# Constant tails of the packed queries and keys written by ScalarE instead of five DMAs, in the three cross attentions of a twelve-layer network

## The chip, the cores and the metric

The kernel runs on one core of one Trainium2 chip. The metric is the device time of one execution in microseconds (us), the median of several runs. A profile of one execution shows when each instruction of each engine ran: TensorE (PE in the rows, its weight loads PEld), VectorE (DVE), ScalarE (ACT), GpSimd (POOL), and the queue of SyncE (SPq), which only issues DMAs here. ScalarE can issue DMAs too (ACTq).

## The reference, cut to what matters

A perceiver: 128 latent rows `x` of 256 columns pass through twelve layers. Three of them (L0, L1, L3) are cross attentions of 16 heads over 12,544 context rows; the other nine aren't touched by the change.

```python
# a cross attention (L0_xattn; L1 adds a mask on the keys, L3 a rotation of the queries)
q = split_heads(x_q @ Wq + bq) * dp_scale        # x_q: layer norm of x, 128 rows, 16 heads of 16
k = split_heads(x_kv @ Wk + bk)                  # x_kv: ctx_1024, 12544 rows
v = split_heads(x_kv @ Wv + bv)
attn = jnp.einsum('bhic,bhjc->bhij', q, k)
attn = jnp.where(causal_mask, neg, attn)
attn = jax.nn.softmax(attn, axis=-1)
o = jnp.einsum('bhij,bhjc->bhic', attn, v)
```

## The kernel before, in words

**Chunks and steps.** `CrossAttention` walks the context in 49 chunks of 256 keys (`NCHUNK`), in 56 steps (`STEPS`). At step `s` the engines project chunk `s` to keys and values. The maxima of the scores of chunk `s - 1` are found from a coarse product. The real scores of chunk `s - 6` (`LAG` is 6) are computed and exponentiated. So the first six steps, 0 to 5, hold projection and maxima only: I call them the run-up. From step 6 on the full loop runs. Step 5 ends with the first shift (minus the maxima), which TensorE turns (line 952) and SyncE sends into the packed queries; the first real score (line 938) stands behind it.

**One step of the run-up**, by engine and line:
- TensorE: the coarse scores of the chunk before (line 889, two batches `d` of 0 and 1), the projection to keys (854), the projection to values (858). The order is batch 0, keys, batch 1, values.
- ScalarE: `act_drain_k` (1099) writes the projected keys with their bias from PSUM to `k_full`; `act_drain_v` (1111) the values; `act_round_context` (1164) rounds the context of chunk `s + 3`; then in steps 0 and 1 `act_low_queries` (1172), in step 2 `act_copy_queries` (1180). In the masked layer L1 the keys are drained by VectorE (1368) instead.
- GpSimd: `split_keys` (1260 high half, 1262 low half), `split_context` (1245, low half of the context).
- VectorE: four reductions (1326) of 1024 columns each; at step 5 `update_shift` (1335 to 1341).
- SyncE: `load_context` (679) of chunk `s + 3`; from step 1 `pack_keys` (691 and 694), eight DMAs that lay the high and low halves of a chunk's keys one below the other in partitions 0 to 95 of one of three buffers `k_packed`; in steps 3 and 4 `pack_queries` (745, 746) for `q_packed`.

**Queues.** Each engine runs its instructions in the order of the code, and a wait holds up everything behind it on that engine. The context load of step 2 stands on SyncE behind the eight `pack_keys` issues of step 1, and those stand behind everything of step 0. On ScalarE the rounding of step 2 (line 1164) waits for the context that this load brings, and the key drain of step 3 stands behind it.

**The tails.** The packed tiles have 128 partitions, and the products use all of them. Partitions 96 and 97 of the queries hold the two parts of the shift; the other rows from 96 on are zero in the queries, while those of the keys are one, so that the product adds the shift. In L1, rows 98 and 99 carry the mask. `fill_tails` (line 721) writes partitions 96 to 127 of both `q_packed` and all three `k_packed` once per layer, by five DMAs of 256 KB from the constants in SBUF, at step 0, after the context load of that step. `pack_keys` and, in L1, `fill_queries` wait on SyncE until all five have landed (`tails_filled` at 80).

Of the kernel before, what the change touches and what calls it, by code (L numbers as in the profile page):

```python
# [8 lines left out]
ACT = mybir.ActivationFunctionType  # L9
F32 = mybir.dt.float32  # L10
# [6 lines left out]
P = 128  # L17
# [4 lines left out]
H = 16  # L22
# [288 lines left out]
def times(ap, m):  # L311

    return ap.unsqueeze(1).broadcast_to([ap.shape[0], m, ap.shape[1]])
# [248 lines left out]
def block_turned(step):  # L562

    return next((b for b in range(BLOCKS) if turn_step(b) == step), None)
# [49 lines left out]
class CrossAttention:  # L614
# [67 lines left out]
    def pack_keys(self, sp, m, quarter):  # L682

        L, s = self.L, m % 3
        if quarter == 0:
            sp.wait_ge(L["k_lo_ready"], m + 1)
            sp.wait_ge(L["tails_filled"], 80)
        if m >= 3:
            sp.wait_ge(L["e_filled"], E_AT["scores", m - 3, 4 + quarter] + 1)
        own = slice(32 * quarter, 32 * quarter + 32)  # L690
        sp.dma_start(self.k_packed[s][0:32, quarter, :, :].rearrange("p d t -> p (d t)").bitcast(F32),
                     self.k_ring[own, m % K_RING, 0, :, :].rearrange("p d t -> p (d t)").bitcast(F32))\
          .then_inc(L[f"packed{s}_{quarter}"], 16)
        sp.dma_start(self.k_packed[s][32:96, quarter, :, :].rearrange("p d t -> p (d t)").bitcast(F32),
                     self.k_ring[own, m % K_RING, :, :, :].rearrange("p a d t -> p a (d t)").bitcast(F32))\
          .then_inc(L[f"packed{s}_{quarter}"], 16)

    def load_key_mask(self, act, m):

        L, s = self.L, m % 3  # L700
        row = self.mask_dram[1:2, m * KEYS:(m + 1) * KEYS].unsqueeze(1).broadcast_to([2, H // 2, KEYS])
        act.dma_start(self.k_packed[s][98:100, :, :, :].rearrange("p q d t -> p (q d) t").bitcast(F32), row)\
           .then_inc(L[f"key_mask_loaded{s}"], 16)
# [10 lines left out]
    def load_shift(self, sp, b):  # L714

        L = self.L
        sp.wait_ge(L["e_drained"], E_AT["turned", b] + 1)
        sp.dma_start(self.q_packed[b % 2][96:98, :, :].bitcast(F32), self.stage_T[32:64, :].bitcast(F32))\
          .then_inc(L["shift_loaded"], 16)

    def fill_tails(self, sp):

        L, tail = self.L, slice(96, P)
        self.wait_first(sp)
        for c in range(2):
            sp.dma_start(self.q_packed[c][tail, :, :].bitcast(F32), times(self.net.const("fill")[tail, :], H))\
              .then_inc(L["tails_filled"], 16)
        for c in range(3):
            sp.dma_start(self.k_packed[c][tail, :, :, :].rearrange("p q d t -> p (q d t)")
                         .rearrange("p (a n) -> p a n", n=P).bitcast(F32), times(self.net.const("ones")[tail, :], H))\  # L730
              .then_inc(L["tails_filled"], 16)

    def pack_queries(self, sp, quarter):

# [13 lines left out]
    def fill_queries(self, sp):  # L748

        L = self.L  # L750
        if self.masked:
            sp.wait_ge(L["tails_filled"], 80)
            sp.dma_start(self.q_packed[0][98:100, :, :].bitcast(F32), times(self.net.const("fill")[0:2, :], H))\
              .then_inc(L["q_packed_ready"], 16)
            sp.dma_start(self.q_packed[1][98:100, :, :].bitcast(F32), times(self.net.const("fill")[0:2, :], H))\
              .then_inc(L["q_repeated"], 16)
# [17 lines left out]
    def sync(self, sp):  # L774
        L, ins = self.L, self.net.ins
# [12 lines left out]
        for step in range(STEPS):  # L788
            m, b = step - LAG + 2, block_turned(step)
            if step + 3 < NCHUNK and step < LAG + 2:  # L790
                self.load_context(sp, step + 3)
            if step == 0:
                self.fill_tails(sp)
            if step == 1:
                self.fill_queries(sp)
            if 1 <= step < 3:
# [117 lines left out]
    def pe_unit(self, pe, m, u):  # L914
# [3 lines left out]
        L, s, half, quarter = self.L, m % 3, u // 4, u % 4  # L918
        unit = E_AT["scores", m, u]
        bank = E_BANK[unit]  # L920
        q = self.q_packed[m // BLOCK % 2]
        if u == 0 and m % BLOCK == 0:
            pe.wait_ge(L["shift_loaded"], 16 * (m // BLOCK + 1))
        if u == 0 and m == BLOCK:
            pe.wait_ge(L["q_repeated"], 32 if self.masked else 16)
        if half == 0:
# [255 lines left out]
    def scalar(self, act):  # L1182
        L = self.L
# [6 lines left out]
            self.act_split_weights(act)  # L1190
        for n in range(3):
            self.act_round_context(act, n)
        if self.masked:
            act.wait_ge(L["mask_stored"], 32)
            self.load_mask(act, 0)
            self.load_mask(act, 1)
        for step in range(STEPS):
            m = step - LAG
# [24 lines left out]
                self.act_low_queries(act, step)  # L1223
            if step == DC:
                self.act_copy_queries(act)
        self.attended.scalar(act)

    def gpsimd(self, pool):
# [1606 lines left out]
```

## Time and profile before

| | |
|---|---|
| median of three runs | 1681.87 us |
| the three runs | 1680.31 to 1682.96 us |
| the profiled execution | 1682.3 us |
| its span in the trace | 1680.5 us (1.8 us lie around it) |
| TensorE busy | 1583.4 us, 94% of the span |
| first real score of L0, L1, L3 | at 48.03, 562.02, 1235.35 us of the span |

The page of the profile gives busy time by engine over the whole span. For a change at the start of three layers the timeline, which lists the instructions of each engine in order of time with the idle time ahead of them and what ended it, is the view to read; the table of stretches gives for each stretch the busy time of the engines and the TensorE clock that was granted.

### The profile page before, as it was taken

To read this page: it belongs to the slowest core of one execution; us is meant where nothing else is said; L and a number is where in the kernel's file an instruction comes from. 1 tells how busy PE (TensorE), PEld (TensorE's weight loads), DVE (VectorE), ACT (ScalarE), POOL (GpSimd) and SP (SyncE) were. 2 spreads that over 40 slices of the span, in tenths; PEclk is the share of its full clock that TensorE was granted. 3 is DMA by queue.
4 is the path that set the end of the run, shared out by engine and by line. 5 is a ranking of instruction groups with operands and counts; after the bars stand their busy time and mean duration, and the time that the engine had idled before them with its cause. 6 is when DMAs were issued, how large, how long until landed. Compare 5 with 4: busy or idle time off the path is not lost. (4 is left out here: it accounts for less than half of the span.)

```text
span 1680.5 us, 48975 instructions
## 1 busy us (share of the span) xinstructions
PE 1583.4 (94%) x20179; PEld 1368.8 (81%) x20179; DVE 1045.0 (62%) x1445; ACT 948.5 (56%) x1812; POOL 693.4 (41%) x627
## 2 busy tenths in 40 slices
PE   7999999999887999999999988998799999999988
PEld 6898888888666889999999775996578998999863
DVE  6667787885346777777777343045676666666622
ACT  3677777777412466666666722352257777777742
POOL 5655555551004645555554000000375555555202
PEclk9999999999978899999999999989999999999997
DMA  6675565554235766555565352970475555655430
GB/s 179 169 194 136 122 139 135 132 124 106 62 116 116 186 184 164 148 144 139 139 150 126 85 208 100 348 274 34 117 183 141 141 128 121 142 133 130 106 105 4
DMA packets 149248, 235.65 MB, mean 140 GB/s; under 512 B 24200, under 2 KB 64516, under 8 KB 148100
## 3 DMA queue, kind: packets, MB, share of 16 engines
q1 hardware_dynamic: 141090, 225.29, 51.4%
q10 hardware_dynamic: 7938, 7.23, 1.7%
q8 instruction: 163, 2.67, 0.7%
q14 instruction: 57, 0.47, 0.1%
HBM read 107.26 MB, written 0.23 MB: 64 GB/s over the span
## 5 line engine op out<-in xcount | busy, mean ns | idle before, releaser
L1326 DVE TENSOR_REDUCE L_xattn_maxima<-L_xattn_ps 128x4 f32<-128x1024 f32 x588 | 691.3, 1219 | 318.7 <-PE L_xattn_ps L889 314.8
L1086 ACT ACTIVATE L_xattn_p_ring<-L_xattn_ps 128x512 f32<-128x512 f32 x1176 | 673.7, 598 | 335.2 <-PE L_xattn_ps L938 319.8
L938 PE MATMUL L_xattn_ps<-L_xattn_q_packed,L_xattn_k_packed 128*128 128x256 f32 x2352 | 450.6, 297 | 5.2 <-ACT L_xattn_p_ring L1086 4.7
L938 PEld LDWEIGHTS L_xattn_ps<-L_xattn_q_packed,L_xattn_k_packed 128*128 128x128 f32 x2352 | 336.2, 190 | 59.5 <-issue 35.9
L980 PE MATMUL L_xattn_ps<-L_xattn_p_ring,L_xattn_v_ring 128*17 128x128 f32 x9408 | 289.3, 273 | 1.0 <-ACT L_xattn_p_ring L1086 1.0
L858 PE MATMUL L_xattn_ps<-L_xattn_w_halves,L_xattn_ctx_halves 128*128 128x256 f32 x1764 | 266.5, 287 | 0.4 <-ACT L_xattn_k_full L1099 0.4
L854 PE MATMUL L_xattn_ps<-L_xattn_ctx_halves,L_xattn_w_halves 128*128 128x256 f32 x1764 | 262.9, 288 | 1.0 <-POOL L_xattn_ctx_halves L1245 1.0
L980 PEld LDWEIGHTS L_xattn_ps<-L_xattn_p_ring,L_xattn_v_ring 128*17 128x17 f32 x9408 | 242.4, 97 | 23.5 <-ACT L_xattn_p_ring L1086 1.6
L1242 POOL TENSOR_TENSOR L_xattn_ctx_halves<-L_xattn_ctx_chunk,consts 128x512 fp32r<-128x512 f32 x129 | 134.2, 1041 | 270.8 <-DMA L_xattn_ctx_chunk<-in_ctx_chunks 192.7
L1260 POOL TENSOR_TENSOR L_xattn_k_ring<-L_xattn_k_full,consts 128x512 fp32r<-128x512 f32 x147 | 153.9, 1047 | 210.4 <-ACT L_xattn_k_full L1099 105.2
L854 PEld LDWEIGHTS L_xattn_ps<-L_xattn_ctx_halves,L_xattn_w_halves 128*128 128x128 f32 x1764 | 235.2, 195 | 4.0 <-issue 1.8
L858 PEld LDWEIGHTS L_xattn_ps<-L_xattn_w_halves,L_xattn_ctx_halves 128*128 128x128 f32 x1764 | 234.8, 193 | 2.6 <-ACT L_xattn_k_full L1099 0.6
L1245 POOL TENSOR_TENSOR L_xattn_ctx_halves<-L_xattn_ctx_chunk,L_xattn_ctx_halves 128x512 fp32r<-128x512 f32 x147 | 189.6, 1290 | 18.4 <-ACT L_xattn_ctx_halves L1164 8.2
L1262 POOL TENSOR_TENSOR L_xattn_k_ring<-L_xattn_k_full,L_xattn_k_ring 128x512 fp32r<-128x512 f32 x147 | 189.5, 1289 | 11.5
L889 PE MATMUL L_xattn_ps<-L_xattn_k_ring,L_xattn_q_hi 32*128 32x256 f32 x2352 | 148.9, 311 | 9.8 <-issue 4.2
L889 PEld LDWEIGHTS L_xattn_ps<-L_xattn_k_ring,L_xattn_q_hi 32*128 32x128 f32 x2352 | 109.6, 185 | 43.3 <-issue 17.8
L1111 ACT ACTIVATE L_xattn_v_ring<-L_xattn_ps 128x512 f32<-128x512 f32 x147 | 87.8, 597 | 51.4 <-PE L_xattn_ps L858 39.8
L1099 ACT ACTIVATE L_xattn_k_full<-L_xattn_ps,weights 128x256 f32<-128x256 f32 x196 | 81.6, 471 | 18.3 <-PE L_xattn_ps L854 18.3
L243 POOL TENSOR_SCALAR L_attn_rstd<-L_attn_mean_var 128x1 f32<-128x1 f32 x4 | 0.9, 221 | 174.3 <-DVE L_attn_mean_var L232 174.3
L1356 DVE TENSOR_TENSOR L_xattn_ps<-L_xattn_ps,L_xattn_factor 128x512 f32<-128x512 f32 x36 | 24.8, 690 | 50.7 <-PE L_xattn_ps L980 50.7
L884 PE MATMUL L_xattn_ps<-L_xattn_fill_rows,L_xattn_fill_terms 2*128 2x512 f32 x392 | 52.5, 501 | 3.6 <-DVE L_xattn_maxima L1326 1.6
L1368 DVE SCALAR_TENSOR_TENSOR L_xattn_k_full<-L_xattn_ps,weights,L_xattn_mask_chunk 128x256 f32<-128x256 f32 x98 | 42.6, 476 | 1.9 <-PE L_xattn_ps L854 1.5
(387 smaller groups left out, 1174.7 us busy)
## 6 DMA issues: line engine op xcount, KB each, us to landing
L_xattn_k_packed<-L_xattn_k_ring SPq DMA_DIRECT2D x588, 128.0 KB, 2.4
L_xattn_ctx_chunk<-in_ctx_chunks SPq DMA_DIRECT2D x147, 256.0 KB, 3.1
L_xattn_k_packed<-L_xattn_k_ring SPq DMA_DIRECT2D x588, 64.0 KB, 2.2
L_ffn_W<-in_experts_W SPq DMA_DIRECT2D x16, 1024.0 KB, 11.8
L_xattn_mask_chunk<-L_xattn_mask ACTq DMA_DIRECT2D x49, 128.0 KB, 3.0
weights<-in_pack_L_attn SPq DMA_DIRECT2D x10, 512.0 KB, 4.9
L_xattn_ctxT<-in_ctxT SPq DMA_DIRECT2D x5, 896.0 KB, 12.9
L_xattn_ctx<-in_ctx SPq DMA_DIRECT2D x5, 896.0 KB, 11.6
```

Of the source, the lines that this page charges most:

```text
L854: last = pe.matmul(L.ps[:, KV_BANK, d * KEYS:(d + 1) * KEYS], wk[:, b, e, d * P:(d + 1) * P], x[:, a, e, :], start=start, stop=stop, skip_ ...
L858: last = pe.matmul(L.ps[:, self.v_bank(n), t * D:(t + 1) * D], x[:, a, e, t * P:(t + 1) * P], wv[:, b, e, :], start=start, stop=stop, skip ...
L889: last = pe.matmul(bank[:, r, k * KEYS:(k + 1) * KEYS], self.q_hi[own, 2 * d + k, :], self.k_ring[own, slot, 0, d, :], start=not self.mask ...
L938: last = pe.matmul(L.ps[:, bank, d * 2 * S:(d + 1) * 2 * S], self.k_packed[s][:, quarter, d, half * P:(half + 1) * P], q[:, 2 * pair:2 * p ...
L980: last = pe.matmul(L.ps[q:q + DH + 1, ACC_BANK, col:col + S], self.v_ring[:, m % V_RING, half, h, :], self.p[t % P_RING][:, at, :], start= ...
L1086: act.activation(self.p[t % P_RING][:, 4 * quarter:4 * quarter + 4, :], L.ps[:, E_BANK[unit], :].rearrange("p (h n) -> p h n", n=S), ACT.Exp)\
L1111: act.activation(self.v_ring[:, n % V_RING, :, :, 0:DH].rearrange("p t h n -> p (t h) n"), L.ps[:, self.v_bank(n), :].rearrange("p (m n) - ...
L1242: pool.tensor_tensor(hi, self.ctx_chunk[c][:, :, :], wide(ones[:, 0:DC], KEYS), ALU.mult)\
L1245: pool.tensor_tensor(lo, self.ctx_chunk[c][:, :, :], hi.bitcast(F32), ALU.subtract)\
L1260: pool.tensor_tensor(hi, k[:, :, :], wide(ones[:, 0:DC], KEYS), ALU.mult).then_inc(L["k_hi_ready"], 1)
L1262: pool.tensor_tensor(lo, k[:, :, :], hi.bitcast(F32), ALU.subtract).then_inc(L["k_lo_ready"], 1)
L1326: dve.tensor_reduce(out[:, 4 * v:4 * v + 4], L.ps[:, M_BANK + 2 * v:M_BANK + 2 * v + 2, :] .rearrange("p b (k n) -> p (b k) n", k=2), AX_X ...
```

## The change

The five DMAs of `fill_tails` are gone. ScalarE writes the same constants: `fill_query_tails` issues two ACTIVATEs (Copy with scale 0.0, so zeros) of 32 partitions by 2048 elements after the three roundings that stand ahead of the steps, and `fill_key_tails` one (Copy of ones) of the same size at the end of steps 1, 2 and 3. `tails_filled` now counts to 5 by ones. `pack_keys` no longer waits for it, since it writes other partitions. The wait has moved to TensorE's first real score, to `load_shift` and `fill_queries` on SyncE (2, the queries alone) and, in L1, to `load_key_mask` on ScalarE.

```diff
     def pack_keys(self, sp, m, quarter):
         if quarter == 0:
             sp.wait_ge(L["k_lo_ready"], m + 1)
-            sp.wait_ge(L["tails_filled"], 80)
...
     def load_key_mask(self, act, m):
+        act.wait_ge(L["tails_filled"], 5)
...
     def load_shift(self, sp, b):
         sp.wait_ge(L["e_drained"], E_AT["turned", b] + 1)
+        sp.wait_ge(L["tails_filled"], 2)
...
-    def fill_tails(self, sp):
+    def fill_query_tails(self, act):
         L, tail = self.L, slice(96, P)
-        self.wait_first(sp)
         for c in range(2):
-            sp.dma_start(self.q_packed[c][tail, :, :].bitcast(F32), times(self.net.const("fill")[tail, :], H))\
-              .then_inc(L["tails_filled"], 16)
-        for c in range(3):
-            sp.dma_start(self.k_packed[c][tail, :, :, :].rearrange("p q d t -> p (q d t)")
-                         .rearrange("p (a n) -> p a n", n=P).bitcast(F32), times(self.net.const("ones")[tail, :], H))\
-              .then_inc(L["tails_filled"], 16)
+            act.activation(self.q_packed[c][tail, :, :], times(self.net.const("ones")[tail, :], H), ACT.Copy, scale=0.0)\
+               .then_inc(L["tails_filled"], 1)
+
+    def fill_key_tails(self, act, c):
+        L, tail = self.L, slice(96, P)
+        act.activation(self.k_packed[c][tail, :, :, :].rearrange("p q d t -> p (q d t)").rearrange("p (a n) -> p a n", n=P),
+                       times(self.net.const("ones")[tail, :], H), ACT.Copy).then_inc(L["tails_filled"], 1)
...
     def fill_queries(self, sp):
         if self.masked:
-            sp.wait_ge(L["tails_filled"], 80)
+            sp.wait_ge(L["tails_filled"], 2)
...
     def sync(self, sp):
-            if step == 0:
-                self.fill_tails(sp)
...
     def pe_unit(self, pe, m, u):
+        if u == 0 and m == 0:
+            pe.wait_ge(L["tails_filled"], 5)
...
     def scalar(self, act):
         for n in range(3):
             self.act_round_context(act, n)
+        self.fill_query_tails(act)
...
             if step == DC:
                 self.act_copy_queries(act)
+            if 1 <= step < 4:
+                self.fill_key_tails(act, step - 1)
```

On SyncE, from the context loads at the start of L0 to the first packed keys, before:

```order
L679 DMA L_xattn_ctx_chunk<-in_ctx_chunks 128x512 [waits L0_xattn_ctx_split]
L726 DMA L_xattn_q_packed<-consts 32x16x128 [waits x_and_consts_loaded]
L726 DMA L_xattn_q_packed<-consts 32x16x128
L729 DMA L_xattn_k_packed<-consts 32x16x128 x3
L679 DMA L_xattn_ctx_chunk<-in_ctx_chunks 128x512 [waits L0_xattn_ctx_split]
L691 DMA L_xattn_k_packed<-L_xattn_k_ring 32x512 [waits L0_xattn_tails_filled,L0_xattn_k_lo_ready]
```

The same place on SyncE now (first line: the loads of steps 0 and 1):

```order
L679 DMA L_xattn_ctx_chunk<-in_ctx_chunks 128x512 [waits L0_xattn_ctx_split] x2
L690 DMA L_xattn_k_packed<-L_xattn_k_ring 32x512 [waits L0_xattn_k_lo_ready]
L693 DMA L_xattn_k_packed<-L_xattn_k_ring 64x1x512
L690 DMA L_xattn_k_packed<-L_xattn_k_ring 32x512
L693 DMA L_xattn_k_packed<-L_xattn_k_ring 64x1x512
```

Five issues and one wait have left the stretch between the context loads and the packing of the first keys.

On ScalarE, from the value drain of step 1 to the key drain of step 3 of L0 (1111 drains values, 1164 rounds context, 1172 and 1180 prepare the queries, 1099 drains keys), before:

```order
L1111 ACTIVATE L_xattn_v_ring<-L_xattn_ps 128x32x16 [waits L0_xattn_v_in_psum]
L1164 ACTIVATE L_xattn_ctx_halves<-L_xattn_ctx_chunk 128x512 [waits L0_xattn_v_in_psum,L0_xattn_ctx_loaded1]
L1172 ACTIVATE L_xattn_p_ring<-L_xattn_p_ring,consts 128x128 [waits L0_xattn_q_lo_ready]
L1172 ACTIVATE L_xattn_p_ring<-L_xattn_p_ring,consts 128x128
L1099 ACTIVATE L_xattn_k_full<-L_xattn_ps,weights 128x256 [waits L0_xattn_k_lo_ready,L0_xattn_k_in_psum]
L1099 ACTIVATE L_xattn_k_full<-L_xattn_ps,weights 128x256
L1111 ACTIVATE L_xattn_v_ring<-L_xattn_ps 128x32x16 [waits L0_xattn_v_in_psum]
L1164 ACTIVATE L_xattn_ctx_halves<-L_xattn_ctx_chunk 128x512 [waits L0_xattn_v_in_psum,L0_xattn_ctx_loaded2]
L1180 ACTIVATE L_xattn_p_ring<-L_xattn_q_hi 128x512 [waits L0_xattn_q_heads_ready]
L1099 ACTIVATE L_xattn_k_full<-L_xattn_ps,weights 128x256 [waits L0_xattn_k_lo_ready,L0_xattn_k_in_psum]
```

The same stretch now (its line numbers are two higher):

```order
L1113 ACTIVATE L_xattn_v_ring<-L_xattn_ps 128x32x16 [waits L0_xattn_v_in_psum]
L1166 ACTIVATE L_xattn_ctx_halves<-L_xattn_ctx_chunk 128x512 [waits L0_xattn_v_in_psum,L0_xattn_ctx_loaded1]
L1174 ACTIVATE L_xattn_p_ring<-L_xattn_p_ring,consts 128x128 [waits L0_xattn_q_lo_ready]
L1174 ACTIVATE L_xattn_p_ring<-L_xattn_p_ring,consts 128x128
L732 ACTIVATE L_xattn_k_packed<-consts 32x2048
L1101 ACTIVATE L_xattn_k_full<-L_xattn_ps,weights 128x256 [waits L0_xattn_k_lo_ready,L0_xattn_k_in_psum]
L1101 ACTIVATE L_xattn_k_full<-L_xattn_ps,weights 128x256
L1113 ACTIVATE L_xattn_v_ring<-L_xattn_ps 128x32x16 [waits L0_xattn_v_in_psum]
L1166 ACTIVATE L_xattn_ctx_halves<-L_xattn_ctx_chunk 128x512 [waits L0_xattn_v_in_psum,L0_xattn_ctx_loaded2]
L1182 ACTIVATE L_xattn_p_ring<-L_xattn_q_hi 128x512 [waits L0_xattn_q_heads_ready]
L732 ACTIVATE L_xattn_k_packed<-consts 32x2048
L1101 ACTIVATE L_xattn_k_full<-L_xattn_ps,weights 128x256 [waits L0_xattn_k_lo_ready,L0_xattn_k_in_psum]
```

A tail (line 732) now stands between the work on the queries and the key drain, at the end of steps 1 and 2; a third one stands at the end of step 3, and two (line 726) ahead of the key drain of step 0.

## Rows read from the trace of the kernel before

**Rows 1.** Page: busy time by engine over the span.

```profile
PE 1583.4 (94%) x20179; PEld 1368.8 (81%) x20179; DVE 1045.0 (62%) x1445; ACT 948.5 (56%) x1812; POOL 693.4 (41%) x627
```

**Rows 2.** Stretches (busy us by engine, then granted TensorE clock): L0, L1, L3.

```profile
32.00:37.00 5.00, 1.99 (x20) 1.89 (x20) 1.45 (x2) 2.27 (x5) 3.06 (x3) 0.98 0.77 185
37.00:42.00 5.00, 5.00 (x25) 4.37 (x25) 4.65 (x7) 1.19 (x3) 4.05 (x5) 0.50 0.83 190
63.00:71.00 8.00, 8.00 (x122) 7.26 (x122) 4.79 (x5) 5.85 (x12) 4.46 (x4) 1.00 0.76 189
...
557.00:562.00 5.00, 5.00 (x32) 4.47 (x29) 3.26 (x3) 0.60 (x1) 4.84 (x5) 0.50 0.62 159
...
1227.00:1232.00 5.00, 3.54 (x33) 3.09 (x33) 3.96 (x7) 1.71 (x4) 4.83 (x5) 1.00 0.71 166
```

**Rows 3.** Timeline, L0 (start, duration, instruction, idle before): SyncE, and VectorE's reductions.

```profile
13.06 5.05 SPq L729 DMA_DIRECT2D L_xattn_k_packed<-consts  x3
...
17.18 4.62 DVE L1326 TENSOR_REDUCE L_xattn_maxima<-L_xattn_ps 128x4 f32<-128x1024 f32 x4 [0.40 <-PE L_xattn_ps L889]
...
22.88 0.57 SPq L691 DMA_DIRECT2D L_xattn_k_packed<-L_xattn_k_ring  x1
...
28.80 0.58 SPq L679 DMA_DIRECT2D L_xattn_ctx_chunk<-in_ctx_chunks  x1
...
35.55 2.35 DVE L1326 TENSOR_REDUCE L_xattn_maxima<-L_xattn_ps 128x4 f32<-128x1024 f32 x2 [3.71 <-PE L_xattn_ps L889]
```

**Rows 4.** Timeline, L0: ScalarE's drains and roundings, GpSimd's split, the first score.

```profile
14.29 0.84 ACT L1099 ACTIVATE L_xattn_k_full<-L_xattn_ps,weights 128x256 f32<-128x256 f32 x2 [3.13 <-PE L_xattn_ps L854]
...
16.58 1.35 POOL L1262 TENSOR_TENSOR L_xattn_k_ring<-L_xattn_k_full,L_xattn_k_ring 128x512 fp32r<-128x512 f32 x1
...
31.91 0.63 ACT L1164 ACTIVATE L_xattn_ctx_halves<-L_xattn_ctx_chunk 128x512 fp32r<-128x512 f32 x1 [4.54 <-DMA L_xattn_ctx_chunk<-in_ctx_chunks]
...
32.97 0.82 ACT L1099 ACTIVATE L_xattn_k_full<-L_xattn_ps,weights 128x256 f32<-128x256 f32 x2
...
48.03 0.40 PE L938 MATMUL L_xattn_ps<-L_xattn_q_packed,L_xattn_k_packed 128*128 128x256 f32 x2
```

**Rows 5.** Groups by line and shape, ScalarE: the same copy at two sizes.

```profile
L1164 ACT ACTIVATE L_xattn_ctx_halves<-L_xattn_ctx_chunk 128x512 fp32r<-128x512 f32 x18 | 10.8, 625 | 12.4 <-DMA L_xattn_ctx_chunk<-in_ctx_chunks 12.3
L1842 ACT ACTIVATE L_xattn_ctx_parts<-L_xattn_ctx 128x1792 fp32r<-128x1792 f32 x5 | 8.5, 1694 | 6.4 <-PE L_xattn_ps L1885 3.6 <-DMA L_xattn_ctx<-in_ctx 2.7
```

**Rows 6.** Timeline, L3: ScalarE, VectorE's reductions of steps 1 and 4, the first score.

```profile
1198.54 1.66 ACT L1164 ACTIVATE L_xattn_ctx_halves<-L_xattn_ctx_chunk 128x512 fp32r<-128x512 f32 x3
...
1205.00 0.84 ACT L1099 ACTIVATE L_xattn_k_full<-L_xattn_ps,weights 128x256 f32<-128x256 f32 x2 [4.81 <-PE L_xattn_ps L854]
...
1207.64 4.62 DVE L1326 TENSOR_REDUCE L_xattn_maxima<-L_xattn_ps 128x4 f32<-128x1024 f32 x4 [1.70 <-PE L_xattn_ps L889]
...
1213.23 0.68 ACT L1172 ACTIVATE L_xattn_p_ring<-L_xattn_p_ring,consts 128x128 f32<-128x128 f32 x2
...
1220.02 0.63 ACT L1164 ACTIVATE L_xattn_ctx_halves<-L_xattn_ctx_chunk 128x512 fp32r<-128x512 f32 x1 [2.19 <-DMA L_xattn_ctx_chunk<-in_ctx_chunks]
...
1223.65 4.62 DVE L1326 TENSOR_REDUCE L_xattn_maxima<-L_xattn_ps 128x4 f32<-128x1024 f32 x4 [1.37 <-PE L_xattn_ps L889]
...
1235.35 0.40 PE L938 MATMUL L_xattn_ps<-L_xattn_q_packed,L_xattn_k_packed 128*128 128x256 f32 x2
```

**Rows 7.** Timeline, L1: mask load behind queued work, value drain, VectorE's chain.

```profile
521.31 0.38 ACT L259 ACTIVATE L_xattn_xnT<-L_xattn_ps 128x256 f32<-128x256 f32 x1 [3.94 <-PE L_xattn_ps L252]
521.33 0.35 ACTq L710 DMA_DIRECT2D L_xattn_mask_chunk<-L_xattn_mask  x1
...
526.30 0.86 DVE L1368 SCALAR_TENSOR_TENSOR L_xattn_k_full<-L_xattn_ps,weights,L_xattn_mask_chunk 128x256 f32<-128x256 f32 x2
...
527.77 0.60 ACT L1111 ACTIVATE L_xattn_v_ring<-L_xattn_ps 128x512 f32<-128x512 f32 x1 [4.52 <-PE L_xattn_ps L858]
...
544.75 4.61 DVE L1326 TENSOR_REDUCE L_xattn_maxima<-L_xattn_ps 128x4 f32<-128x1024 f32 x4
```

## The prediction, made before the changed kernel ran

> **What bounds the kernel now.** TensorE is busy 94% of the span [rows 1]. In the full loop it has no gap: 8.00 of 8.00 us at full clock in the stretch from 63 us [rows 2]. A change that only touches the run-up of a layer can't shorten that loop. It can only let it begin earlier, and the loop then carries the shift to its end, since nothing in it stands on a fixed time. So the measure is the time of the first real score of each of the three layers, and I read the timeline backwards from it.
>
> The views in their order. First the timeline of VectorE. In the run-up a step takes 5.02 us, 4.62 of reductions and 0.40 for the turn to the next batch [rows 3]. I call the start of a step's first reduction t1 (step 1) to t4 (step 4). In L0, t1 is 17.18 and t4 would be 17.18 + 3 x 5.02 = 32.24, but it is 35.55, after 3.71 us of idle time. Then the timeline of ScalarE: it stood 4.54 us until 31.91, waiting for a context load, and only then came to the key drain of step 3, at 32.97 [rows 4]. From the start of that drain to t4 it is 35.55 - 32.97 = 2.58 us (drain, split on GpSimd, coarse product). Then the timeline of SyncE, for why the load was late: it was issued at 28.80, behind eight packing issues that began only at 22.88, though their keys were ready at 16.58 + 1.35 = 17.93 [rows 3, 4]. What they waited for were the five tail DMAs, whose last three took SyncE from 13.06 to 18.11 to issue, and then had to land.
>
> L3 shows the same in small: 2.19 us of waiting for the load, and 1.37 us of idle ahead of t4 in place of 0.40 [rows 6]. In L1 nothing of it reaches VectorE. Its row at 544.75 has no idle time ahead of it [rows 7], because there VectorE drains the keys itself and is the slowest engine of the step.
>
> **What is removed.** Packing of the first keys can start at about 18 instead of 22.88, and the context load behind it moves as much, from 28.80 to about 23.9; with the 3.1 us between issue and use (28.80 to 31.91) it is there at 27.0. ScalarE asks for it at about 27.7 (below), so this wait goes altogether. In L3 the load moves alike. Left alone, the removal would bring t4 in L0 to 32.24, 3.3 us earlier, and in L3 by 1.37 - 0.40 = 1.0 us.
>
> **What is added: five ACTIVATEs per layer.** No row has one of 2048 elements per partition. The nearest are the same SBUF copy at 1792 (1694 ns) and at 512 (625 ns) [rows 5]: 0.835 ns an element, so 1.694 + 256 x 0.835/1000 = 1.91 us each. Bounds: 1.69 below (the row of 1792) and, if a source that repeats 128 elements or a write to 32 partitions ran at half the rate, 3.8 above. I take 1.91, because cost follows the elements per partition in every ScalarE row. Queued ones overlap: three of 0.62 take 1.66 [rows 6], so 0.09 to 0.10 each.
>
> *The two query tails*, ahead of the first key drain: 2 x 1.91 less three overlaps is 3.55 us. ScalarE was idle there for 3.13 in L0, 4.52 in L1 and 4.81 in L3 [rows 4, 6, 7]. L1 and L3 hide them; in L0 they delay the key drain of step 0, and with it t1, by 0.42, to 17.60.
>
> *The key tail of step 1.* The work on the queries ends at t1 + 6.27 (1213.91 - 1207.64 in L3) [rows 6]. The tail runs from t1 + 6.18 to t1 + 8.09, and the key drain of step 2 starts at t1 + 8.00 at the earliest, with t3 = t1 + 8.00 + 2.58 = t1 + 10.58. Undisturbed it would be t1 + 10.04. So this tail costs 0.54 in both layers, where keys are drained by ScalarE.
>
> *The key tail of step 2.* The same sum with one copy of 512 elements (0.62, as in [rows 5]) where two short ones (0.68) stood gives the drain of step 3 at t2 + 7.94, and t4 no earlier than t2 + 10.52 = t1 + 15.54. The other path is t3 + 5.02 = t1 + 15.60. The second decides, so this tail is hidden, by 0.06 only. *That of step 3* ends about t4 + 1.8, when the next keys just come out of TensorE: 0 to 0.2, and the drain of step 4 has slack there. I take 0.
>
> Together t4 is t1 + 15.60: in L0 17.60 + 15.60 = 33.20, 2.35 earlier than 35.55. In L3 it is 1207.64 + 15.60 = 1223.24, 0.41 earlier than 1223.65.
>
> **From t4 to the first score.** It took 48.03 - 35.55 = 12.48 us in L0 [rows 3, 4] and 1235.35 - 1223.65 = 11.70 in L3 [rows 6]. The difference is TensorE's clock: after the gap in L0 (1.99 busy of 5 us) it was granted half, 1.2 GHz, for the stretch from 37 us, while L3 stayed at 2.4 GHz with 3.54 busy of 5 at worst [rows 2]. With the gap gone the run-up of L0 looks like that of L3, so I take 11.70: another 0.78 us. Bounds: 0 and 0.78.
> The Trainium skill, in TensorE: Matmul & The Clock Gate, section HAM oscillation, says that waits for data between groups of matmuls bring the slow clock back. By that rule too the 0.78 comes with the gap. L1 speaks against counting on it: it had half clock from 557 to 562 us [rows 2] without a late load on VectorE's path, which is a rival below.
>
> **The moved waits** cost nothing. The third key tail ends near 35 in L0, and TensorE's first score, which waits for it, comes at 45; `load_shift` asks for the query tails, done at about 14.8. The ScalarE wait in L1 is on its own earlier writes. Five issues fewer on SyncE give slack and no time in L1.
>
> **L1** by itself: its query tails end before the value drain at 527.77 wants ScalarE. Its mask loads are issued by ScalarE behind them, though. They were issued at 521.33, 0.02 us after the first of four queued ACTIVATEs began [rows 7]. So the sequencer runs at least four ahead. If it ran no further, two more would hold the issue until the second of them is done, at about 522.2: 0.9 late. The mask was wanted at 526.30. With 0.35 of issue and the 3.1 us that the larger context load took to be used, it is there at about 525.7. So 0, with a bound of 0.9.
> The Trainium skill, in Advanced Engine Details and Errata, section Engine Queue Depths, gives eight entries for ScalarE. By it the six ACTIVATEs fit and the issue isn't held at all; no row here shows more than four.
>
> **The sum.** L0 2.35 + 0.78 = 3.13; L3 0.41; L1 0. That is 3.5 us, from the profiled 1682.3 us to 1678.8. This execution was 0.4 above the median of 1681.87, so the median goes to 1678.4. Own range of this case: 2.7 to 4.5 saved, 1677.4 to 1679.2.
>
> **Rivals.**
> (a) *The clock falls anyway, somewhere else in L0's run-up*, as it did in L1. A stretch of 5 us at half clock, all busy, holds 2.5 us of work at full clock [rows 2], so up to 2.5 of the 3.5 are lost, in the middle 1.9: 1680.3. For it: TensorE still waits for the shift in step 5. Against it: L3 has the same wait and kept its clock.
> (b) *The first score comes earlier but the loop doesn't.* Something else, such as SyncE's packing in steps 5 to 8, sets the loop's start. Then 0 to 0.8 saved, about 1681.5. Against it: the stretch from 63 us has no gap on TensorE, and SyncE gains slack.
> (c) *Slower: a tail takes far longer than its elements say.* The place is ScalarE in steps 0 to 2 of L0 and L3. With T for one tail, L0's t1 moves by 2 (T - 1.91) and t4 by 3 (T - 1.91); L3's t4 by 1 (T - 1.91) while its query tails are hidden. The gain of 3.5 is eaten at 4 (T - 1.91) = 3.5, so at T = 2.8. At T = 3.8 it is 3.5 - 4 x 1.9 = -4.1 and about 1 more because L3's query tails come out of cover: 1687. Against it: no ScalarE row is slower than by its elements. For it: no row has this shape.
> (d) *More is saved:* the tails run nearer 1.69, or the freed DMA traffic speeds the rest. t3 in both layers then gains 0.2, t1 in L0 0.4, and all of the removal would come through at most: 3.3 + 0.78 + 1.0 = 5.1, 1676.8.
>
> **How the numbers follow.** Forecast 0.62, (a) 0.13, (b) 0.10, (c) 0.07, (d) 0.08. The range leaves out (c) and the ends of (b) and (d): 1676.9 to 1681.8. A measurement of this kernel tells about 0.2%, 3.4 us, from no change, so the line is at 1678.5, in the middle of my forecast. Faster by more than that: half of the forecast, a little over, and (d), 0.42. Slower: (c) and a trace of noise, 0.08. Within 0.2%: the rest, 0.50.
>
> **What would show it.** In L0: rows of line 726 and 732 of 1.9 us each; key drain of step 0 at 14.7; no wait of ScalarE for a context load; t3 near 28.2 (0.54 later than two undisturbed steps after t1), t4 near 33.2, full clock from 37 to 42 us, first score at 44.9. In L3: t4 0.4 us earlier counted from the layer's start. In L1: the first score as long after the layer's start as before. I am wrong if a tail isn't near 1.9 us, if L0's first score comes before 43.5 or after 46, or if the full loop begins to show gaps on TensorE.

## The result, and the profile after

The changed kernel takes 1676.22 us in the median of 20 runs, beside 1681.64 us for the kernel before on the same chip: ratio 0.9976, 95% interval 0.9968 to 0.9984, which is 4.0 us less (2.7 to 5.4; the two medians alone lie 5.4 us apart, at the edge of that). Timed again later it was 1676.31 us beside 1680.47, ratio 0.9970 (0.9959 to 0.9981). The forecast was 3.5 us less. On the median of 1681.87 us from which it was made, the first ratio gives 1677.8 us, in the range; the raw median lies 0.7 us below the range's low end. The profiled span is 1673.7 us.

The page has fewer packets and bytes (149248 and 235.65 MB before), and more of ScalarE than in [rows 1]:

```profile
PE 1579.2 (94%) x20179; PEld 1364.2 (82%) x20179; DVE 1037.2 (62%) x1445; ACT 977.5 (58%) x1827; POOL 694.1 (41%) x627
...
DMA packets 141328, 231.72 MB, mean 138 GB/s; under 512 B 23960, under 2 KB 56596, under 8 KB 140180
```

ScalarE's timeline in L0 (start, duration, instruction, idle before it), to be laid beside [rows 4]. L726 are the query tails, L732 the key tails, L1101 the key drains, L1166 the rounding of the context:

```profile
10.69 3.72 ACT L726 ACTIVATE L_xattn_q_packed<-consts 32x2048 fp32r<-32x2048 f32 x2
14.43 0.84 ACT L1101 ACTIVATE L_xattn_k_full<-L_xattn_ps,weights 128x256 f32<-128x256 f32 x2
...
22.35 0.62 ACT L1166 ACTIVATE L_xattn_ctx_halves<-L_xattn_ctx_chunk 128x512 fp32r<-128x512 f32 x1
...
23.57 1.91 ACT L732 ACTIVATE L_xattn_k_packed<-consts 32x2048 fp32r<-32x2048 f32 x1
25.51 0.84 ACT L1101 ACTIVATE L_xattn_k_full<-L_xattn_ps,weights 128x256 f32<-128x256 f32 x2
...
27.35 0.62 ACT L1166 ACTIVATE L_xattn_ctx_halves<-L_xattn_ctx_chunk 128x512 fp32r<-128x512 f32 x1
...
28.51 1.91 ACT L732 ACTIVATE L_xattn_k_packed<-consts 32x2048 fp32r<-32x2048 f32 x1
30.45 0.84 ACT L1101 ACTIVATE L_xattn_k_full<-L_xattn_ps,weights 128x256 f32<-128x256 f32 x2
```

Each key tail is 1.91 us, the two query tails 3.72 together. The rounding at 27.35 has no idle time ahead of it, where 4.54 us stood before. Now VectorE in L0, beside [rows 3]; the last four rows are the reduction of the maxima and the three small operations of the first shift:

```profile
17.29 4.62 DVE L1331 TENSOR_REDUCE L_xattn_maxima<-L_xattn_ps 128x4 f32<-128x1024 f32 x4 [1.59 <-PE L_xattn_ps L889]
22.29 4.63 DVE L1331 TENSOR_REDUCE L_xattn_maxima<-L_xattn_ps 128x4 f32<-128x1024 f32 x4 [0.38 <-PE L_xattn_ps L889]
28.11 4.62 DVE L1331 TENSOR_REDUCE L_xattn_maxima<-L_xattn_ps 128x4 f32<-128x1024 f32 x4 [1.19 <-PE L_xattn_ps L889]
33.11 4.62 DVE L1331 TENSOR_REDUCE L_xattn_maxima<-L_xattn_ps 128x4 f32<-128x1024 f32 x4 [0.38 <-PE L_xattn_ps L889]
37.76 0.30 DVE L1340 TENSOR_REDUCE L_xattn_maxima<-L_xattn_maxima 128x16 f32<-128x80 f32 x1
38.10 0.49 DVE L1344 TENSOR_SCALAR L_xattn_stage<-L_xattn_maxima 128x16 fp32r<-128x16 f32 x1
38.62 0.97 DVE L1345 SCALAR_TENSOR_TENSOR L_xattn_stage<-L_xattn_maxima,L_xattn_stage 128x16 fp32r<-128x16 f32 x1
39.62 0.18 DVE L1346 TENSOR_TENSOR L_xattn_shift<-L_xattn_stage 128x16 f32<-128x16 f32 x1
```

The four first rows are t1 to t4. The 3.71 us ahead of t4 are gone; 1.19 us stand ahead of t3 in their place, 0.8 more than the usual 0.38. TensorE's clock (the figure right behind the five counts, 1.00 is 2.4 GHz) stays up where [rows 2] had 0.50, and the first score of L0 comes at 44.14 us instead of 48.03:

```profile
32.00:37.00 5.00, 4.82 (x43) 4.07 (x42) 4.62 (x5) 3.35 (x4) 3.79 (x4) 1.00 0.82 183
37.00:42.00 5.00, 4.17 (x39) 3.74 (x37) 3.94 (x7) 1.71 (x4) 4.78 (x5) 1.00 0.22 67
```

In L3 the first score comes 39.76 us after the layer's first context load is issued (1190.67 to 1230.43), before 40.53 (1194.82 to 1235.35). The two run-ups together give 3.89 + 0.77 = 4.66 us. The spans differ by more, 6.8 us. Of the other 2.1 us, 1.34 lie in L1's run-up and the rest in stretches that the change doesn't touch. The next table shows how far both wander: e5, whose L1 has the code of the kernel before, has a run-up of 44.10 us there, not 45.50.

The table holds the time from a layer's first context load to its first score, for L0 from the start of the span, and the two long stretches between the run-ups (first score of L0 to L1's first load, first score of L1 to L3's). All in us, from the traces:

| kernel | L0 t1 | L0 t4-t1 | L0 first score | L1 run-up | L3 run-up | L0 to L1 | L1 to L3 | ratio to before |
|---|---|---|---|---|---|---|---|---|
| before | 17.18 | 18.37 | 48.03 | 45.50 | 40.53 | 468.5 | 632.8 | 1 |
| changed | 17.29 | 15.82 | 44.14 | 44.16 | 39.76 | 468.2 | 634.1 | 0.9976 |
| changed, again | 17.81 | 15.83 | 44.65 | 44.09 | 39.33 | 468.8 | 633.2 | 0.9970 |
| e1 | 17.68 | 16.26 | 45.62 | 43.95 | 38.58 | 467.4 | 634.6 | 0.9975 |
| e2 | 17.21 | 15.00 | 44.92 | 44.53 | 39.43 | 470.5 | 631.6 | 0.9981 |
| e3 | 17.76 | 15.01 | 43.50 | 46.80 | 38.56 | 468.8 | 633.1 | 0.9965 |
| e4 | 17.34 | 19.02 | 47.45 | 44.05 | 42.75 | 469.4 | 633.2 | one run |
| e5 | 17.13 | 18.01 | 46.85 | 44.10 | 40.71 | 467.7 | 634.8 | one run |
| e6 | 17.04 | 15.04 | 42.80 | 45.22 | 38.57 | 469.1 | 633.0 | 0.9969 |
| e7 | 17.53 | 15.84 | 43.60 | 41.70 | 37.87 | 467.9 | 632.3 | 0.9936 |
| e10 | 17.30 | 15.03 | 42.39 | 42.18 | 36.93 | 468.2 | 632.5 | 0.9930 |
| e11 | 17.32 | 19.10 | 47.33 | 42.97 | 38.70 | 467.3 | 636.0 | 0.9963 |

### The profile page after: what moved, and what is told of

Same layout as the page of the kernel before. It is cut to its first block and busy times, and to the rows that moved or that the text cites. A ratio compares the mean times of both kernels' runs of the same rounds, so it can differ in the third digit from the quotient of the medians.

```text
span 1673.7 us, 49007 instructions
## 1 busy us (share of the span) xinstructions
PE 1579.2 (94%) x20179; PEld 1364.2 (82%) x20179; DVE 1037.2 (62%) x1445; ACT 977.5 (58%) x1827; POOL 694.1 (41%) x627
## 5 line engine op out<-in xcount | busy, mean ns | idle before, releaser
L1101 ACT ACTIVATE L_xattn_k_full<-L_xattn_ps,weights 128x256 f32<-128x256 f32 x196 | 81.8, 472 | 6.2 <-PE L_xattn_ps L854 6.0
```

## The experiments

**The wait or the transfers: e1.** The kernel before, with the wait moved and the five DMAs left where they were.

```diff
     def pack_keys(self, sp, m, quarter):
         if quarter == 0:
             sp.wait_ge(L["k_lo_ready"], m + 1)
-            sp.wait_ge(L["tails_filled"], 80)
...
     def pe_unit(self, pe, m, u):
+        if u == 0 and m == 0:
+            pe.wait_ge(L["tails_filled"], 80)
```

> The kernel before with the five tail DMAs where they were, but the wait for them taken from pack_keys and put where the changed kernel has it: ahead of the first real score on TensorE, of load_shift and of the key-mask loads. ScalarE writes nothing. Theory (what cost the kernel before its time was the wait for the DMAs to land, at one place of SyncE's queue): pack_keys of chunk 0 starts near 18 us in L0, the context load of step 2 near 23, ScalarE's rounding doesn't wait, t3 is t1+10.04, t4 is t1+15.06 (32.2), the first score of L0 comes near 43.2 us (the changed kernel: 44.14), and the time is 1 to 2 us below the changed kernel's, about 1675 us. Rival (the five transfers themselves, 2.5 times the bytes of a pack, crowd the queues and the packed copies that come after): SyncE's issues stretch from 0.6 towards 2 us each, the context load of step 2 lands late all the same, t4 stays over 33, and the time is between the two kernels', 1678 to 1681 us.

Measured: 1676.22 us, ratio 0.9975 (0.9960 to 0.9990), the same as the changed kernel's. My theory had the time nearly right and the trace of L0 wrong. There t4 is t1 + 16.26, against 18.37 before and 15.06 undisturbed, so the wait cost 2.1 us, and with the DMAs still there another 1.2 stayed. SyncE's and ScalarE's timelines in L0 show where:

```profile
11.41 1.41 SPq L727 DMA_DIRECT2D L_xattn_q_packed<-consts  x2
12.86 5.01 SPq L730 DMA_DIRECT2D L_xattn_k_packed<-consts  x3
17.91 1.59 SPq L679 DMA_DIRECT2D L_xattn_ctx_chunk<-in_ctx_chunks  x1
19.54 1.53 SPq L690 DMA_DIRECT2D L_xattn_k_packed<-L_xattn_k_ring  x1
...
24.94 2.15 SPq L693 DMA_DIRECT2D L_xattn_k_packed<-L_xattn_k_ring  x1
```

```profile
23.22 0.63 ACT L1167 ACTIVATE L_xattn_ctx_halves<-L_xattn_ctx_chunk 128x512 fp32r<-128x512 f32 x1 [0.38 <-DMA L_xattn_ctx_chunk<-in_ctx_chunks]
...
30.30 0.63 ACT L1167 ACTIVATE L_xattn_ctx_halves<-L_xattn_ctx_chunk 128x512 fp32r<-128x512 f32 x1 [2.45 <-DMA L_xattn_ctx_chunk<-in_ctx_chunks]
```

Issues that take 0.6 us elsewhere take about 1.5 to 1.8 here up to 21.1 us, and one takes 2.15 at 24.94. The context load of step 2 is issued at 27.13, beside 23.16 in the changed kernel, and ScalarE still waits 2.45 us for it. The first part of this stands while the tails are in flight. The last of them landed at 22.40, though, and a long issue near this place is in every L0: 1.45 us at 25.41 in the kernel before, 1.25 us at 26.26 in the changed kernel, where it stands behind the context load and delays nothing that is waited for. So the 1.2 us came with the DMAs, but how much of it their transfers made and how much the long issue that now fell ahead of the load isn't shown. In L3 t4 is t1 + 15.04: there the DMAs cost nothing, while ScalarE's tails cost the changed kernel 0.8 us. The first score of L0 comes 1.5 us later than in the changed kernel and that of L3 1.2 us earlier, which fits two equal times.

**Later DMAs for the keys: e2.** Query tails on ScalarE, key tails by DMA in step 3.

```diff
+            if step == 3:
+                self.fill_key_tails(sp)
...
-            if 1 <= step < 4:
-                self.fill_key_tails(act, step - 1)
```

> The changed kernel with the query tails on ScalarE as they are, but the three key tails fetched by DMAs again, issued by SyncE in step 3 behind that step's query packing, and waited for only at the first real score and the key-mask loads. Theory (each key tail on ScalarE pushes the K drain of the next step; in the changed kernel the one of step 1 costs 0.78 us in L0 and in L3): the VectorE idle of 1.19 us ahead of t3 falls to 0.38, t4 is t1+15.06 (32.4), the DMAs issue at about 32 to 34 us and land by 41, and the first score of L0 comes near 43.4. L3 gains as much. Time 1.5 us below the changed kernel's, about 1674.7. Rival (the late DMAs delay the query packing's landing or the context loads behind them, and the first score waits for them): first score of L0 at 44 or later, time that of the changed kernel or up to 1 us above it.

Measured: 1676.82 us, ratio 0.9981 (0.9966 to 0.9997). The first half of the theory held: t4 is t1 + 15.00, no idle ahead of t3. Then the rival did. TensorE's timeline of L0, key projection and first score:

```profile
43.27 0.74 PE L858 MATMUL L_xattn_ps<-L_xattn_ctx_halves,L_xattn_w_halves 128*128 128x256 f32 x4 [0.81 <-DMA L_xattn_q_packed<-L_xattn_p_ring]
44.92 0.79 PE L944 MATMUL L_xattn_ps<-L_xattn_q_packed,L_xattn_k_packed 128*128 128x256 f32 x2 [0.91 <-DMA L_xattn_q_packed<-L_xattn_stage_T]
```

```profile
42.00:47.00 5.00, 3.28 (x17) 2.87 (x18) 2.17 (x2) 0.60 (x1) 4.72 (x5) 0.69 0.75 173
47.00:52.00 5.00, 4.98 (x26) 4.23 (x26) 2.35 (x2) 3.01 (x6) 2.32 (x2) 0.50 0.89 224
```

The packed queries land late behind the tails, TensorE waits twice, and the clock falls to 0.50 behind that. So step 3 isn't a free place for these transfers either; others weren't tried.

**Another place for the key tails: e3 and e6.** e3 puts them behind the key drain of the same step in all layers, e6 in L0 and L3 alone.

```diff
             self.act_drain_k(act, step)
+            if 1 <= step < 4:
+                self.fill_key_tails(act, step - 1)
             self.act_unit(act, m, 2)
```

> The changed kernel with the three key tails still on ScalarE in steps 1, 2 and 3, but right behind the K drain of the step, ahead of its V drain, where ScalarE of L0 sat idle for 2.09 us in step 1 (19.76 to 21.85), and no longer behind the rounding of the context. Theory (an ACTIVATE of 1.91 us costs what it pushes, and here it fits the gap): the K drain of step 2 starts near 24.0, t3 is t1+10.04 with 0.38 us of idle ahead of it, t4 is t1+15.06 (32.4), the first score of L0 near 43.4, and L3 gains 0.75 us as well; time about 1674.7 us, 1.5 below the changed kernel's. Rival (the V drain comes later by what the tail overruns the gap, and the rounding and the V projection behind it are late instead): t3 as in the changed kernel, t1+10.8, and a time within 0.5 us of the changed kernel's.

> The key tails behind the K drain of steps 1, 2 and 3 in L0 and L3, as in e3_tails_after_drain, but in the masked layer L1 where the changed kernel has them, behind the rounding of the context. Theory (in e3_tails_after_drain the place gained 1.0 us or so in L0 and L3 against the changed kernel, t3 and t4 without idle, and lost in L1, where VectorE waited 1.33 us for TensorE after 529 us, because the V drain stood behind the tail): first score of L0 near 43.2 to 43.6, L3 start to first score 38.6, L1 start to first score 44.2 to 45.5 instead of 46.80, and a time 0.5 to 1.5 us below that of e3_tails_after_drain, about 1674.3. Rival (L1's longer run-up was made by the clock, which dips there in every kernel, and is given back later): L1's pace of reductions is regular, yet the time is that of e3_tails_after_drain within its interval.

Measured: e3 1675.15 us, ratio 0.9965 (0.9952 to 0.9978); e6 1674.79 us, 0.9969 (0.9957 to 0.9981). In both, t4 is t1 + 15.0 in L0 and the L3 run-up is 38.6 instead of 39.76: the 1.91 us of ACTIVATE fit the gap between key and value drain, and the 0.8 us that the tail of step 1 had pushed is back; another 0.3 lies behind t4 and is explained below. In L1, e3 does cost VectorE a wait (1.33 us at 532.96), and e6 has its even pace again. The time didn't follow: e6's clock in L1 stayed low longer (0.50 and 0.59 in 552 to 562 us), its run-up took 45.22, and the ratios are the same within their intervals. The rival on L1 holds as far as these traces go. Against the changed kernel neither place is a difference that the intervals settle.

**Longer tails: e4.** Each key tail written twice.

```diff
                 self.fill_key_tails(act, step - 1)
+                act.wait_ge(self.L["tails_filled"], 2 * step + 1)
+                self.fill_key_tails(act, step - 1)
```

> The changed kernel with each key tail written twice in a row on ScalarE, so that its cost is 3.8 us instead of 1.91. Theory (the tail of step 1 is at the edge of its cover and every further microsecond of steps 1 and 2 goes to VectorE's period): L0 t3 is 1.9 us later against t1 than in the changed kernel (t1+12.7), t4 3.8 later (t1+19.6), the first score 3.8 to 5.7 later (48 to 50 us); in L3 t4 is later by 1.9 to 3.8. Time 7 to 11 us above the changed kernel's, 1683 to 1687. Rival (there is cover left in steps 2 and 3, VectorE's reductions and the clock set the pace): t4 is less than 2.5 us later and the time stays under 1681.

Measured: 1682.97 us in one run. In L0 t3 is t1 + 12.76, 1.94 later than in the changed kernel, as expected. t4 is t1 + 19.02, 3.20 later and not 3.8, and the first score 3.31. In L3 the first score is 2.99 later, in L1 not at all. That is 6.3 us of run-ups; the one run is 6.8 us above the changed kernel's median. The tail of step 1 has no cover left, and that of step 2 some 0.6 us: ScalarE had been idle for 0.50 us between the two, ahead of the value drain at 26.85.

**The clock: e5.** The kernel before with 13 matmuls of zeros in the gap of L0.

```diff
             if step < LAG - 1:
+                if step == 4 and self.first:
+                    L.keep_busy(pe, E_BANKS[0], 13)
                 self.pe_batch(pe, step, 0)
```

> The kernel before, tails by DMA and the wait in pack_keys as they were, with 13 further matmuls of zeros (128x512, into a free PSUM bank, their result unused) on TensorE in step 4 of L0 alone, ahead of that step's first batch, where TensorE of the kernel before sat idle for 3.25 us (31.75 to 35.01). Theory (0.8 us of what the changed kernel gained in L0 is TensorE's clock, which fell to 0.50 in 37 to 42 us after that idle): t4 stays near 35.5, granted clock 1.00 in 37 to 42 and 42 to 47, the first score of L0 comes near 47.2 us instead of 48.03. Rival (the clock doesn't matter there, since VectorE and the shift set the pace): full clock, but the first score still at 48.0 within 0.2.

TensorE's stretches in L0:

```profile
32.00:37.00 5.00, 4.92 (x36) 3.08 (x34) 1.86 (x2) 2.09 (x6) 3.46 (x3) 1.00 0.79 178
37.00:42.00 5.00, 3.73 (x32) 3.22 (x28) 4.86 (x7) 2.06 (x5) 4.25 (x5) 1.00 0.75 177
```

Full clock, and from t4 (35.14) to the first score (46.85) 11.71 us instead of 12.48. The clock was worth 0.77 us. The further 0.41 us by which the score is early came with t4; the wait for the context load was 0.35 us shorter in this trace. The one run took 1681.33 us, which doesn't tell 1.2 us from none.

**What the sum didn't have: e7, e11.** After e5 one thing was open. The clock explains 12.48 to 11.71, but the changed kernel takes 11.03 in L0 and 11.02 in L3, where the clock was full before as well and it took 11.70. GpSimd's timeline of the changed kernel in L0, against the VectorE rows above:

```profile
37.27 1.29 POOL L1267 TENSOR_TENSOR L_xattn_k_ring<-L_xattn_k_full,L_xattn_k_ring 128x512 fp32r<-128x512 f32 x1
38.52 1.04 POOL L1247 TENSOR_TENSOR L_xattn_ctx_halves<-L_xattn_ctx_chunk,consts 128x512 fp32r<-128x512 f32 x1
39.64 1.30 POOL L1250 TENSOR_TENSOR L_xattn_ctx_halves<-L_xattn_ctx_chunk,L_xattn_ctx_halves 128x512 fp32r<-128x512 f32 x1
```

L1344 began at 38.10 and ended at 38.59, GpSimd's first one here at 38.56. L1345 began at 38.62, 0.10 after GpSimd's next, and ended at 39.59, that one at 39.56. Both take 0.17 to 0.20 alone. The kernel before had the same, with other partners:

```profile
40.83 0.89 DVE L1339 TENSOR_SCALAR L_xattn_stage<-L_xattn_maxima 128x16 fp32r<-128x16 f32 x1
41.76 0.17 DVE L1340 SCALAR_TENSOR_TENSOR L_xattn_stage<-L_xattn_maxima,L_xattn_stage 128x16 fp32r<-128x16 f32 x1
41.97 1.14 DVE L1341 TENSOR_TENSOR L_xattn_shift<-L_xattn_stage 128x16 f32<-128x16 f32 x1
```

GpSimd's operations there ran 40.65 to 41.69 and 41.77 to 43.08. A small VectorE operation of this kind that begins while GpSimd works on a tensor ends with GpSimd's. The reduction L1340 doesn't: it ran 37.76 to 38.06 beside GpSimd's first one and took 0.30. The Trainium skill, in SBUF — State Buffer, section Who interferes with whom, has this as a rule: the two engines share a pair of ports, a VectorE instruction with two SBUF inputs or in a two-port mode needs it, and the later one blocks for the whole of the other. The rows here agree: L1345, with two inputs, and L1344 were held, the reduction with its one input wasn't. Which mode L1344 ran in no row tells. e7 takes the overlap of L1345 away in the changed kernel, e11 those in the kernel before:

```diff
         for step in range(NCHUNK):
             if step < LAG:
                 split_keys(step)
+                if step == LAG - 2:
+                    pool.wait_ge(L["stage_ready"], 1)
                 split_context(step + 2)
```

> The changed kernel with one wait more: GpSimd doesn't begin the split of context chunk 6 (in step 4 of each layer) before VectorE's shift of block 0 is done. In all traces so far a small operation of that shift (128x16, 0.17 to 0.20 us alone) that met a GpSimd tensor operation ended with it: in the changed kernel L1345 ran 38.62 to 39.59 and GpSimd's 38.52 to 39.56. Theory (a VectorE operation of this kind waits until GpSimd's has ended, and this is the term that made the end of the run-up 0.7 us shorter than figured): L1345 takes 0.17 to 0.2, the shift 1.2 to 1.3 us instead of 2.04 in L0 and 2.05 in L3, the first scores come 0.7 to 0.8 earlier against t4 in both (10.3 instead of 11.03), GpSimd's split starts 0.3 to 0.5 later, and the time is 1 to 1.5 us below the changed kernel's, about 1674.9. Rival (GpSimd's later split delays the keys of chunk 5 and the context, or something else stretches the small operations): the first score comes as late as in the changed kernel, 44.1, and the time is the same or 0.5 us more.

> The kernel before with nothing but the added wait of e7_gpsimd_after_shift: GpSimd begins the split of context chunk 6 when the shift of block 0 is done. Theory (the collision of VectorE's small operations with GpSimd's is a cost of its own, which was there before the change and depends only on how the two engines happen to line up): the shift of L0 takes near 1.0 to 1.3 us instead of 2.61, that of L3 as much instead of 2.63, both first scores come 1.3 to 1.6 us earlier (L0 near 46.5, L3 start to first score near 39.0), the clock of L1 stays at 1.00 and its start to first score is 41.7 instead of 45.5, and the time is 5.5 to 7 us below that of the kernel before, about 1675. Rival (the gain of the added wait needs the changed kernel's timing): less than 3 us of gain.

VectorE, then GpSimd, in L0 of e7:

```profile
38.35 0.49 DVE L1346 TENSOR_SCALAR L_xattn_stage<-L_xattn_maxima 128x16 fp32r<-128x16 f32 x1
38.88 0.17 DVE L1347 SCALAR_TENSOR_TENSOR L_xattn_stage<-L_xattn_maxima,L_xattn_stage 128x16 fp32r<-128x16 f32 x1
39.09 0.17 DVE L1348 TENSOR_TENSOR L_xattn_shift<-L_xattn_stage 128x16 f32<-128x16 f32 x1
```

```profile
39.34 1.04 POOL L1247 TENSOR_TENSOR L_xattn_ctx_halves<-L_xattn_ctx_chunk,consts 128x512 fp32r<-128x512 f32 x1 [0.53 <-DVE L_xattn_shift L1348]
```

The length of the shift (from L1340's start to L1346's end, in each kernel's own numbering) sets the time from t4 to the first score:

| shift, us | t4 to first score | seen in |
|---|---|---|
| 2.69 to 2.71 | 11.68 to 11.70 | before (L3), e1 (L0) |
| 2.02 to 2.05 | 11.00 to 11.03 | changed and changed again, L0 and L3 |
| 1.73 to 1.74 | 10.73 to 10.75 | e3, L0 and L3 |
| 1.24 | 10.21 to 10.23 | e7, L0 and L3 |
| 0.94 | 10.05 to 10.06 | e10, L0 and L3 |

Four run-ups of L0 and L3 don't follow it, for reasons of their own: L0 of the kernel before (2.61, 12.48) and L0 of e11 (0.95, 10.91; granted clock 0.81 from 37 to 42 us) had the slow clock, and in e2 (1.75, 12.71 in L0; 1.74, 11.51 in L3) the packed queries were waited for.

Times: e7 1669.80 us, ratio 0.9936 (0.9922 to 0.9951); e11 1675.10 us, 0.9963 (0.9949 to 0.9977). e7 is some 6 us below the changed kernel where I had expected 1 to 1.5. L0 and L3 gave their 0.8 each behind t4. I had left out L1, where the shift shrank too and TensorE then kept its clock. The stretches from 547 us, first of the changed kernel, then of e7:

```profile
547.00:552.00 5.00, 2.89 (x30) 2.50 (x28) 4.83 (x9) 0.87 (x2) 3.86 (x4) 0.96 0.12 33
552.00:557.00 5.00, 4.90 (x40) 4.29 (x37) 3.61 (x4) 0.63 (x2) 4.80 (x5) 0.70 0.47 126
```

```profile
547.00:552.00 5.00, 4.12 (x40) 3.25 (x38) 4.83 (x11) 0.87 (x2) 3.83 (x5) 1.00 0.20 56
552.00:557.00 5.00, 5.00 (x46) 4.47 (x47) 4.54 (x7) 2.53 (x5) 4.84 (x5) 1.00 0.72 185
```

L1's shift took 0.91 us instead of 2.38, and its run-up fell from 44.16 to 41.70. That makes 0.8 + 0.8 + 2.5 = 4.1 of the 6 us. Another 1.1 came ahead of t1 in L3, ahead of the place where the edit acts in that layer. The key projection of step 0 took 1.77 us there and not 2.63. In the second trace of the changed kernel it took 1.78 as well, but t1 came only 0.4 us sooner than in the first, since VectorE was held by GpSimd once more, in its work on the queries:

```profile
1200.25 1.61 DVE L1413 TENSOR_TENSOR L_xattn_q_hi<-L_xattn_p_ring,consts 128x256 fp32r<-128x256 f32 x2
1201.79 1.50 DVE L1417 TENSOR_TENSOR L_xattn_p_ring<-L_xattn_p_ring 128x256 fp32r<-128x256 f32 x1
```

In the first trace these took 0.76 and 0.42, in e7 0.76 and 1.26. So this 1.1 us is the clock at the layer's entry, together with how the two engines line up behind it, and not the edit. The rest lies between the layers, and I have no cause for it. e11 gave 1.83 us in L3 and 2.5 in L1, where the clock still fell to 0.66 in 557 to 562 us. In L0 it gave 0.7, because ScalarE's two waits for context loads were 0.7 us longer in that trace (1.24 and 4.99 instead of 1.01 and 4.54). Its time is 6.2 us below the kernel before, as forecast: the added wait needs nothing of the change.

**Both together: e10**, e6 and e7 in one.

> e6_drain_place_not_masked and e7_gpsimd_after_shift in one: key tails behind the K drain in L0 and L3, and GpSimd's split of chunk 6 behind the shift. Theory (the two gains are of different terms and add): L0 first score near 42.7, L3 start to first score near 37.9, time 2 to 2.5 us below the changed kernel's, about 1674. Rival (what is saved in the run-ups is given back by the clock, as in the late-DMA kernel where it fell to 0.50 behind the first score): first scores as forecast, a dip of the clock behind them, and a time within 0.7 us of the changed kernel's.

Measured: 1668.37 us, ratio 0.9930 (0.9916 to 0.9943), no dip behind the first scores: granted clock 1.00 in 42 to 52 and in 1220 to 1240 us. It beats both kernels, the one before by 11.8 us; against e7 the intervals overlap.

**The same kernel twice: e9.** The changed kernel, unaltered.

> The changed kernel once more, as it is, for how far two traces of one program differ. Theory (the run-ups of L0 and L3 are set by waits, and repeat; the stretch of L1 and what lies between the layers differ by how long the clock stays low): L0 first score within 0.5 us of 44.14, nearly all of it from the first reduction's time, t3 - t1 10.82 and t4 - t1 15.82 again within 0.05, L3 start to first score within 0.1 of 39.76, shift operations stretched by the same amounts, and L1 start to first score anywhere between 43.9 and 45.5. Rival (the stretched small operations line up by chance): L1345 takes 0.2 us in one of the two layers, and the first score comes 0.8 us earlier, or another operation is stretched and it comes 0.6 later.

t3 - t1 is 10.83 and t4 - t1 15.83 (10.82 and 15.82 in the first trace), the shift 2.02 us with the same two operations stretched. What moved is t1, by 0.52 us. The L3 run-up is 0.43 shorter, more than I expected, 0.39 of it ahead of its t1.

## Why the prediction was right, point by point

- **What is removed** was right in L0: the wait of 4.54 us is gone. e1 refines why. Of the 3.3 us, 2.1 were the wait, and 1.2 stayed as long as the DMAs were issued at all, which the prediction didn't separate. That the DMAs went, and not only their wait, counts in L0 alone.
- **1.91 us for a tail** holds in every row. The copy that repeats 128 elements into 32 partitions goes by elements per partition. Rival (c) is out, but its condition was real: e4, with 3.8 us for a key tail, is back at the time of the kernel before.
- **Query tails, 0.42.** Not seen. The key drain of step 0 moved by 0.14 (14.29 to 14.43), since the roundings ended sooner, and t1 by 0.11. t1 ranges over 17.13 to 17.68 in the kernels without these tails and 17.04 to 17.81 in those with them.
- **Key tail of step 1, 0.54.** Mis-sized, it is 0.78: t3 is t1 + 10.82. The drain starts at t1 + 8.22 and not 8.00, because the tail and the drain behind it don't overlap (23.57 + 1.91 = 25.48, drain at 25.51) and the steps ahead overlap less than I let them.
- **Key tail of step 2, hidden.** Right: t4 is t3 + 5.00. With the two errors against each other, t4 in L0 is 33.11, forecast 33.20.
- **L3, 0.41.** Mis-sized, t4 came 0.09 earlier from the layer's start. The term above takes 0.24 of the difference. My slope, one for one for the key tails, was wrong as well: the tail of step 2 was hidden by 0.06 only, so past that both tails count. e4 moved t4 by 3.2 us for 1.91 more in L0, and by 3.2 from the layer's start (3.6 from t1) in L3.
- **The clock, 0.78.** Right; e5 measures 0.77, and rival (a) didn't come. Nor did (b): from L0's first score to L1's first load it is 468.2 us, beside 468.5 before, so the loop carried the gain on, and TensorE is busy 8.00 of 8.00 us from 63 us as before.
- **From t4 to the first score, 11.70.** The step that failed: 11.03 and 11.02. I took the shift as fixed. In the kernel before the key drain paced t4, and two of the small operations met GpSimd's; in the changed kernel VectorE paces itself, and the meeting costs less. That is 0.68 us in each of L0 and L3.

So L0 is 2.44 + 0.77 + 0.68 = 3.89 and L3 0.09 + 0.68 = 0.77. The forecast of 3.13 + 0.41 was low by 1.1 us, with an unforeseen gain of 1.36 that covered a tail dearer than thought. The mechanism of L0 up to t4 and of its clock was right. In L3 the foreseen terms give 0.09 of the 0.77 us, and that the total lies near the measured 4.0 us is in part luck.

- **L1, 0.** Its reductions keep their pace. The mask loads were issued at 517.07, 0.01 us after the first of six queued ACTIVATEs began, so the bound of 0.9 us is empty. The run-up was 1.3 us shorter than before, but 43.95 to 45.50 is what traces show with L1's order of work nearly untouched (44.10 in e5, which is untouched there). 1.2 of the 1.3 lie behind t4, where TensorE's clock falls in both kernels.

## What to carry to other kernels

A transfer that no one needs yet can cost by the wait behind it and by the place that its issue takes in a queue; try moving the wait first, which here brought as much as the whole change. When work is moved to another engine, look for the gap where its length fits between two pieces that others wait for. Before costing a chain of small VectorE operations, lay GpSimd's timeline beside it: an operation of 0.2 us that takes 1 us and ends with GpSimd's is waiting for it, and one semaphore can give that back.

## What the runs showed of the hardware that was not expected

- VectorE operations of 128x16, 0.17 to 0.20 us alone, took up to 1.14 us where they began beside a GpSimd tensor operation, and ended with it, within 0.04 us. Casts of 128x512 to bf16 took 1.27 and 1.50 us in e1 and 0.41 in the changed kernel. The reductions from PSUM, 1.22 us each, weren't stretched.
- A shift shorter by some 1.5 us in L1 left TensorE 4.12 us busy of 5 instead of 2.89, and the clock of the next stretch stayed at 2.4 GHz in e7.
- Of SyncE's 1476 to 1491 DMA issues, which mostly take 0.3 to 0.7 us, 88 to 116 took over 0.9 us in each trace, with tail DMAs or without. Those of the key tails in L0 took 1.25 to 1.97 us before, and one in e1 2.15 us when all tails had landed. What makes an issue long isn't shown.
